# One k rotation moved to VectorE, and a division moved ahead of GpSimd's k rotations

## The reference

```python
qh = rope(layernorm(x) @ wq.T);  kh = rope(ctx @ wk.T);  vh = ctx @ wv.T
scores = qh @ kh.T / 8, masked to j <= i and j >= i - 64
x = x + tanh(g_xattn) * (softmax(scores) @ vh) @ wo.T
probs = softmax(layernorm(x) @ router_w.T);  gate = the 4 largest of probs, else 0
x = x + tanh(g_ffn) * (sum of shared experts + sum of gate * expert(layernorm(x)))
```

## Time and profile before

| | us |
|---|---|
| median of three runs | 506.68 |
| the profiled execution | 505.21 |
| its span | 503.4 |
| TensorE busy in the span | 492.7 (98%) |
| VectorE busy | 359.9 (71%) |
| ScalarE busy | 311.0 (62%) |
| GpSimd busy | 266.7 (53%) |

### The profile page before, as it was taken

The page is one execution under the profiler, slowest core; times in us unless marked ns, Lnnn a source line. Parts: engine busy times, 40 slices in busy tenths (PEclk is TensorE's granted clock), DMA queues, the critical chain, the costliest instruction groups (busy, mean ns, idle before and its releaser), DMA issues.

```text
span 503.4 us, 14340 instructions
## 1 busy us (share of the span) xinstructions
PE 492.7 (98%) x5386; PEld 406.3 (81%) x5386; DVE 359.9 (71%) x1159; ACT 311.0 (62%) x861; POOL 266.7 (53%) x206
## 2 busy tenths in 40 slices
PE   8998999999999999999999999999999999999997
PEld 5787888888888888888888787777878887888885
DVE  6988958765797667887976858787667665745454
ACT  5596785656766664866776856666446545644442
POOL 4999999999998999997899311001000100000000
PEclk9999999999999999999999999999999999999999
DMA  7462114230132310310421156326702570255021
GB/s 268 121 206 79 46 44 138 66 79 19 38 108 43 100 35 7 80 38 4 101 60 33 30 192 231 83 33 185 239 9 35 183 236 10 35 182 205 0 35 50
DMA packets 50996, 46.37 MB, mean 92 GB/s; under 512 B 30224, under 2 KB 33424, under 8 KB 50928
## 3 DMA queue, kind: packets, MB, share of 16 engines
q1 hardware_dynamic: 50928, 45.46, 31.5%
HBM read 32.72 MB, written 2.24 MB: 69 GB/s over the span
## 4 chain that ended last, share of the span: by engine, by line
PE 76%; POOL 13%; issue 3%; ACT 3%; DVE 3%; DMA 1%; SPq 0%; DVEq 0%; POOLq 0%; ACTq 0%
PE ring L1193 53%; PE psS L1193 10%; PE psTO L1423 5%; POOL arena L549 4%; PE psS L1384 3%; POOL arena L554 3%; POOL prob L562 3%; PE psTO L1404 2%; POOL wl L570 2%; PE psTO L1400 2%; ACT prob L760 1%; POOL arena L543 1%; DMA raw<-in_w 1%; POOL arena L540 1%; POOL xTl L575 0%
## 5 line engine op out<-in xcount | busy, mean ns | idle before, releaser
L1193 PE MATMUL ring<-xTh,wh 128*128 128x512 f32 x268 | 108.2, 404 | 0.4 <-DVE lex L946 0.2
L1193 PE MATMUL ring<-xTh,wl 128*128 128x512 f32 x268 | 105.3, 393 | 0.0
L1193 PE MATMUL ring<-xTl,wh 128*128 128x512 f32 x268 | 105.1, 392 | 0.0
L562 POOL TENSOR_TENSOR prob<-prob,rinv 128x512 f32<-128x512 f32 x62 | 66.2, 1072 | 15.2 <-DVE rinv L1094 14.9
L675 ACT ACTIVATE oTh<-prob 128x512 fp32r<-128x512 f32 x64 | 40.4, 632 | 54.3 <-PE ring L1193 26.8
L987 DVE TENSOR_TENSOR oTl<-prob,oTh 128x512 fp32r<-128x512 f32 x64 | 44.0, 688 | 37.1 <-ACT oTh L675 36.7
L596 POOL TENSOR_TENSOR rstd<-vare,mhalf 128x4 f32<-128x4 f32 x8 | 9.2, 1155 | 103.3 <-DVE vare L884 103.3
L659 ACT ACTIVATE sneg<-ring 128x512 f32<-128x512 f32 x72 | 42.9, 595 | 33.2 <-PE ring L1193 33.1
L979 DVE TENSOR_TENSOR prob<-sneg,arena 128x512 f32<-128x512 f32 x64 | 44.1, 690 | 24.9 <-ACT sneg L659 24.8
L1193 PEld LDWEIGHTS ring<-xTh,wh 128*128 128x128 f32 x268 | 50.3, 188 | 12.5 <-issue 0.9
L1193 PEld LDWEIGHTS ring<-xTh,wl 128*128 128x128 f32 x268 | 50.3, 188 | 11.2
(11 more groups left out here) (146 smaller groups left out, 1172.8 us busy)
## 6 DMA issues: line engine op xcount, KB each, us to landing
arena<-gate_scratch SPq DMA_DIRECT2D x64, 256.0 KB, 6.3
raw<-in_e SPq DMA_DIRECT2D x18, 256.0 KB, 2.7
raw<-in_w SPq DMA_DIRECT2D x16, 256.0 KB, 3.8
arena<-arena SPq DMA_DIRECT2D x24, 128.0 KB, 2.3
pT<-pT SPq DMA_DIRECT2D x96, 32.0 KB, 2.0
arena<-arena SPq DMA_DIRECT2D x10, 256.0 KB, 3.3
out<-x SPq DMA_DIRECT2D x16, 128.0 KB, 6.1
x<-in_x SPq DMA_DIRECT2D x3, 512.0 KB, 4.5
```

What stands on the lines that cost most here:

```text
L562: pool.tensor_tensor(prob[:, c % BUFS, :, :], prob[:, c % BUFS, :, :], rinv[:, c % BUFS, :].unsqueeze(2).to_broadcast([P, TT, P]), ALU.mul ...
L1193: last = pe.matmul(out, a, b, start=start and i == 0 and j == 0, stop=stop and i == n - 1 and j == 2, skip_group_check=check)
```

## The change

Five edits:

- Piece 15's low part moves from GpSimd to VectorE (`LO_ON_P`).
- The function that did the first q pair of unit 0 on VectorE takes any q or k first pair, and it is called for k of unit 2 as well, in step 6, ahead of the low part of piece 10.
- GpSimd no longer rotates that pair.
- In GpSimd's loop, at k = 2, the division of step c - 1 now comes ahead of both k pairs; before it stood between them.
- GpSimd's adds of the second pairs of q of unit 0 and of k of unit 2 wait until VectorE's add of the first pair is done.

```diff
-LO_ON_P = (2, 4, 5, 6, 12, 13, 14, 15)
+LO_ON_P = (2, 4, 5, 6, 12, 13, 14)
...
                 pool.wait_ge(qk_mul[i], rotated("qk"[i], n, pair))
+                if pair and (i, n) in ((0, 0), (1, 2)):
+                    pool.wait_ge(qk_rot[i], rotated("qk"[i], n, 0))
...
-                if k == 2 and u + 1 < UNITS:
-                    rotate_pair(1, u + 1, 0)
                 if c > OPENED + 1 and not before_q(c - 1):
                     divide(c - 1)
+                if k == 2 and 2 < u + 1 < UNITS:
+                    rotate_pair(1, u + 1, 0)
                 if k == 2 and u + 1 < UNITS:
                     rotate_pair(1, u + 1, 1)
...
-            def join_first():
+            def join_here(kind, u):
+                i = "qk".index(kind)
+                part = swap[:, i, 0, :]
+                dst = qT[:, u % 2, 0, :] if kind == "q" else kT[:, u % 2, 0, W:]
+                if u == 0:
+                    dve.wait_ge(in_sin, 16)
+                dve.wait_ge(qk_swap[i], rotated(kind, u, 0))
                 link(dve.tensor_tensor(part, part, sin[:, :], ALU.mult))
-                dve.wait_ge(qk_mul[0], 1)
-                dve.tensor_tensor(dst, dst, part, ALU.add).then_inc(qk_rot[0], 1)
+                dve.wait_ge(qk_mul[i], rotated(kind, u, 0))
+                dve.tensor_tensor(dst, dst, part, ALU.add).then_inc(qk_rot[i], 1)
...
                 if c == OPENED + 1:
+                    join_here("k", 2)
                     do(("w", 10))
```

More of the change, by code:

```diff
@@ L919, in rotate @@
                                       ALU.mult).then_inc(qk_mul[i], 1)
-            def join_first():
-                part, dst = swap[:, 0, 0, :], qT[:, 0, 0, :]
-                dve.wait_ge(in_sin, 16)
-                dve.wait_ge(qk_swap[0], 1)
+            def join_here(kind, u):
[5 more added lines that the diff above has]
+                dve.wait_ge(qk_swap[i], rotated(kind, u, 0))
                 link(dve.tensor_tensor(part, part, sin[:, :], ALU.mult))
-                dve.wait_ge(qk_mul[0], 1)
-                dve.tensor_tensor(dst, dst, part, ALU.add).then_inc(qk_rot[0], 1)
+                dve.wait_ge(qk_mul[i], rotated(kind, u, 0))
+                dve.tensor_tensor(dst, dst, part, ALU.add).then_inc(qk_rot[i], 1)
             def router(b):
@@ L1111, in _ @@
             rotate(("q", 0), 0)
-            join_first()
+            join_here("q", 0)
             rotate(("q", 0), 1)
```

## The result

| | before | after |
|---|---|---|
| median, us | 506.71 (4 runs, 506.62 to 507.21) | 514.07 (4 runs, 513.06 to 515.20) |
| profiled execution, us | 505.21 | 513.06 |
| its span, us | 503.4 | 511.2 |

Slower: the medians lie 7.4 us apart, and the ratio taken over all executions is 1.0153, with its 95% interval 1.0132 to 1.0173. 3.55 us were forecast. The sign was right and the size less than half of what came: 514.07 lies outside the range given, 506.8 to 512.5.

The account below looks back on a forecast made before the run. TensorE was taken to set the end, with GpSimd almost full. Terms of 0.15 + 1.3 + 1.2 + 0.9 = +3.55 us on 506.68 gave 510.2 us, range 506.8 to 512.5.

Parts of the forecast that it names:

- What bounds the kernel: From 93 to 200 us TensorE is always busy and sets the end; GpSimd has only some 4% in hand.
- Part 1: Division ahead of both k pairs, units 2 to 14: context waits of +1.3 and +1.2 us, weight residues +0.9.
- short waits: TensorE waits before scores where a VectorE weight residue meets the first k pair: three units, 0.3 each, +0.9 us.
- rival C: Slower than forecast: TensorE waits before the scores in each of eleven units, 0.2 us more each, 512.4 us; chance 12%.
- The working of unit 6: Reciprocal done at 133.83, division from 133.91, context at 144.25; TensorE begins k of unit 8 at 144.3, not 142.97.
- Part 2, the join: Unit 2's first k pair on VectorE: 1.67 us won at 49.03, VectorE late afterwards, 0.54 back at 85.66; sum +0.15 us.
- TensorE is thus 0.7 later there: At TensorE's wait at 59.39, VectorE's late maximum makes it 0.7 us later, whatever was won at 49.03.
- Part 3: Residue 15 on VectorE, between the rotations of q and k of unit 4, plus the added GpSimd waits: taken as nothing.
- at most 0.9 us of it shows on VectorE: Residue 15 takes 0.66 to 1.66 us in VectorE's 0.72 us wait; over 1 us of TensorE slack follows the maximum.

Follow-up runs that it names:

- e5: Kernel after with ten 128x128 identity matmuls of extra work in TensorE's 1.5 us gap; 509.90 us, ratio 1.0087 to the kernel before.
- e1: Kernel after with residue 15 back on GpSimd; 511.97 us, ratio 1.0126 to the kernel before.
- e4: Kernel after with reciprocal 4u + 1 on VectorE ahead of the two score maxima of its step; 506.48 us, ratio 1.0012 to the kernel before.
- e3: Kernel before with only the first k pair of unit 2 moved to VectorE, plus the added GpSimd waits; 508.21 us, ratio 1.0042.
- e6: Kernel before with only residue 15 moved to VectorE; 504.41 us, ratio 0.9980.
- e10: Kernel before with residue 15 on VectorE, the division ahead of both k pairs and reciprocal 4u+1 ahead of the score maxima; 504.83 us, ratio 0.9977.
- e11: Kernel before, GpSimd rotating unit 2's first k pair before its second q pair, router's residue eight steps later, residue 15 on VectorE; 504.77 us.
- e12: Kernel after with unit 2's first k pair back on GpSimd and no added waits; 509.46 us, ratio 1.0063 to the kernel before.
- e2: Kernel before with only the division moved ahead of both k pairs; 509.14 us, ratio 1.0071.
- e9: e7 with GpSimd rotating unit 2's first k pair before its second q pair, and the router's residue moved to step 19; 506.16 us.
- e8: Kernel before with GpSimd rotating unit 2's first k pair ahead of its second q pair; 506.79 us, ratio 1.0012.
- e7: Kernel before with the division ahead of both k pairs and reciprocal 4u+1 ahead of the two score maxima; 505.16 us, ratio 0.9988.

## Why the prediction was right and wrong, step by step

**What bounds the kernel:** right. TensorE sets the end, GpSimd has nothing to give, and all that was lost stands in places where one of them waits.

**Part 1, division ahead of k, +3.4:** right in mechanism, place and size. Measured in the kernel after: 1.24 and 1.30 (forecast 1.3 and 1.2), short waits 1.1 (0.9). TensorE has these short waits in five units, not in eleven, as rival C had it. The working of unit 6 came out step by step. The kernel after's VectorE and GpSimd there:

```profile
138.01 0.17 DVE L1099 RECIPROCAL rinv<-rsum 128x4 f32<-128x4 f32 x1
```

```profile
135.74 2.41 POOL L543 TENSOR_TENSOR arena<-arena 128x1024 f32<-128x1024 f32 x1
138.26 1.04 POOL L564 TENSOR_TENSOR prob<-prob,rinv 128x512 f32<-128x512 f32 x1
139.26 1.29 POOL L549 TENSOR_TENSOR arena<-arena,sin 128x512 f32<-128x512 f32 x1
140.63 1.71 POOL L556 TENSOR_TENSOR arena<-arena 128x512 f32<-128x512 f32 x1
...
146.36 2.37 POOL L577 TENSOR_TENSOR xTl<-craw,xTh 128x1024 fp32r<-128x1024 f32 x1
```

TensorE is 4.35 us later here than in the kernel before. With that taken off, the division starts at 133.91 (forecast 133.91), the first pair is done at 137.99 (137.9), the context at 144.38 (144.25), and TensorE starts at 144.53 (144.3). What the forecast did not have is that GpSimd, itself late, came free only at 138.15, with its reciprocal 0.03 us later: it had its waits in other units, 1.84 us in unit 4 (2.0 forecast) and between 0.1 and 2.3 in the later ones, which were to be small.

**Part 2, the join, +0.15:** the waits were sized rightly (measured -0.18: 0.45 in the opening, 0.63 back at 88.16), and the chain went nearly as worked out: VectorE's maximum 1.1 us later (53.85 against 52.73), ScalarE's exponentials and copies behind it. TensorE met this one job before the values matmuls, in a gap of 1.54 at 58.55, ended by this copy:

```profile
57.88 0.57 ACT L783 ACTIVATE pT<-psTO 128x512 f32<-128x512 f32 x1
```

The failed step is "TensorE is thus 0.7 later there", which prices the new gap by its length alone. The gap also let the clock fall to 0.50 behind it: 1.5 us in the profile, 2.0 by e5 against e1, 1.7 by e4's two groups. Nothing in the trace of before showed this price, since its own gap of 1.67 at 49.03 was followed by a full clock. I can say that filling the gap removes it (e5). I can't say why a gap of the same length at 49 is harmless (the rows show only that TensorE was fully busy behind it, and e3's profile that the same gap at 58 can be harmless too), nor why this one costs in 4 of 10 executions of one kernel and 4 of 4 of another. That it differs from execution to execution at all fits the Trainium skill ("TensorE: Matmul & The Clock Gate", section "What's actually happening"): what the clock goes by is free-running and doesn't start anew with the kernel, so the same program meets it at another phase each time. e4's ten executions, six full and four not, agree; no run here shows the phase itself.

**Part 3, residue 15, 0:** wrong. The failed step is "at most 0.9 us of it shows on VectorE, and the score maximum that it would make late is followed by over 1 us of slack on TensorE. I take nothing." Measured: 0.52 + 1.18 = 1.7 us on TensorE, 1.4 by e1. Both halves fail. It took 2.69 us, not at most 1.66, because the GpSimd instruction it met was of double size (2.38), and the bound had been read where GpSimd ran single ones. And the slack was used up: after part 1 reciprocal 13 stands ahead of k's first pair, so lateness on VectorE passes over GpSimd to the scores. In e6, without the other parts, it gained 1.0. Which of the two prices falls due goes with the clock in these traces. In all five profiles with residue 15 on VectorE and a full clock (e5, e6, e10, e11, e12) it was issued ahead of GpSimd's rotation and took 0.69 to 0.75 us, in e5 although the join is there; in both profiles with the lower clock (the kernel after and e4) it came 0.24 us behind and took 2.69. So the 1.7 us are, as far as these profiles show, a second cost of the same fall of the clock. Executions that were not profiled can't tell.

**The parts were summed as if apart.** Alone they are +0.71%, +0.42% and -0.20% (e2, e3, e6), together 0.93%; the whole is 1.53%. The difference of 3 us is, for 2.4 of it, residue 15's change from -1.0 to +1.4. Some 0.5 of this is the 0.54 at 85.66, which e2 and e6 each win and the whole can win only once: with the division moved, the residue gains 0.4 and not 1.0 (e12 against e2, a difference within their intervals). For the rest VectorE comes to the residue behind GpSimd, and the moved division passes the damage on.

**Still open:** 0.7 us by which the first matmuls on real data started later. They hang on the first weights and context, whose DMAs let ScalarE begin at 6.51 and 7.38 instead of 6.00 and 6.71; in the profiles of the other kernels the lateness of TensorE at 10 us lay between -0.1 and +0.9, so it may be chance. And 0.7 us at 102.35, where TensorE stood in the middle of a job that waits for nothing there. e9 has the same stall (0.6) at the same matmul, e8 and e12 one of 0.3, and e5 one of 1.4 near 169; the others have none of that size. No run here was aimed at it.

## What to carry to other kernels

- Price a gap on the engine that sets the end not by its length alone: look at the granted clock of the stretch behind it, over several executions, and fill the gap with idle matmuls once, as in e5, to see what it hides.
- Where two engines exclude each other for whole instructions, a moved instruction costs what the longest neighbour takes if it comes second, and nearly nothing if it comes first. A place where the two issue within 0.3 us of each other has two prices, as residue 15 has here; keep both in the range, and don't add parts that shift such a place as if they were apart.
- Before a waiting instruction is moved ahead in an ordered queue, move what it waits for ahead in its own queue. Here one reciprocal of 0.17 us per unit turned 3.6 us lost (e2) into 0.6 won (e7).

## What the hardware showed that I had not expected

- After TensorE had been busy for 0.46 and 1.42 us in two stretches of 2 us, its clock stood at 0.50 for about 3 us of full work; a 128x256 matmul then took 0.41 instead of 0.28 us:

```profile
62.98 0.41 PE L1199 MATMUL ring<-wh,xTl 128*128 128x256 f32 x1
...
64.16 0.28 PE L1199 MATMUL ring<-wh,xTl 128*128 128x256 f32 x1
```

- It does so in some executions only: the same instructions of e4 took 505.27 us in one execution, at a mean clock of 1.000, and 508.10 in another, at 0.993.
- VectorE's subtraction of 128x512 took 0.69 us when issued 0.06 us ahead of a GpSimd instruction and 2.69 us when issued 0.24 us behind it, while GpSimd lost 0.48 in the first case and nothing in the second.
